# Two attention and expert layers on one core: other places for the first batches of the second attention, and the shared expert between the experts

## What is computed

```python
x = x + tanh(g_xattn[0]) * L0_xattn(layernorm(x), ctx)            # 16 heads of 8 rows, with projections
x = x + tanh(g_ffn[0])   * L0_ffn(layernorm(x))                   # 32 experts, 4 per token, 128 places each, and a shared one
x = x + tanh(g_xattn[1]) * L1_xattn(layernorm(x), ctx, ctx)       # 8 heads of 16 rows, no projections
x = x + tanh(g_ffn[1])   * L1_ffn(layernorm(x))                   # 8 experts, 2 per token, and a shared one
# L0_ffn: an expert takes at most 128 tokens
xe = zeros((E, CAP, D)).at[e_flat, pos].set(flat[tok], mode='drop')
h = relu2(einsum('ecd,ehd->ech', xe, up_w)); ye = einsum('ech,edh->ecd', h, down_w)
routed = (ye[e_flat, pos] * topk_w).reshape(T, K, D).sum(axis=1)
shared = relu2(hidden @ shared_up_w.T) @ shared_down_w.T
# L1_xattn
sm = softmax(einsum('bhdq,bhdl->bhql', qh, kh) * scale); ret = einsum('bhql,bhdl->bhdq', sm, vh)
```

## Time and profile before

| what | value |
|---|---|
| median of 3 runs | 784.0 us (779.7 to 788.89) |
| the profiled execution's own time | 784.32 us |
| its span in the trace | 782.5 us |
| TensorE busy, share of the span | 668.5 us, 85% |
| VectorE | 522.0 us, 67% |
| ScalarE | 378.4 us, 48% |
| GpSimd | 321.2 us, 41% |

### The profile page before, as it was taken

How to read it: one execution, slowest core, us unless ns; L and a number is a source line. 1 busy time by engine, 2 the same in 40 slices (tenths; PEclk the granted TensorE clock), 3 DMA queues, 4 the chain that set the end, 5 groups by cost and what they waited for, 6 DMA issues and landing times.

```text
span 782.5 us, 13620 instructions
## 1 busy us (share of the span) xinstructions
PE 668.5 (85%) x4737; PEld 349.8 (45%) x4738; DVE 522.0 (67%) x1252; ACT 378.4 (48%) x630; POOL 321.2 (41%) x337
## 2 busy tenths in 40 slices
PE   3899999999999899788646788799977999888896
PEld 1233333333333357567413344344423566666673
DVE  3889888888895798255267888796837733323236
ACT  2058878888776443243315566575502213333320
POOL 3534353534011101662578877621100057667430
PEclk9999999999999999799957999999999999999999
DMA  6834343544311700455346767786430022222127
GB/s 166 176 88 120 97 117 98 137 139 126 98 46 32 256 14 3 126 159 176 111 128 183 192 195 204 195 187 160 134 117 28 1 63 83 65 74 75 45 85 268
DMA packets 106362, 93.23 MB, mean 119 GB/s; under 512 B 25205, under 2 KB 92954, under 8 KB 106104
## 3 DMA queue, kind: packets, MB, share of 16 engines
q1 hardware_dynamic: 93600, 67.67, 31.6%
q0 software_dynamic: 8352, 18.74, 8.3%
q10 hardware_dynamic: 4344, 5.97, 2.8%
HBM read 50.63 MB, written 16.01 MB: 85 GB/s over the span
## 4 chain that ended last, share of the span: by engine, by line
PE 56%; DVE 14%; issue 11%; POOL 10%; DMA 4%; ACT 2%; SPq 2%; another core or an unknown queue 0%; ACTq 0%; POOLq 0%; DVEq 0%
PE O L443 9%; PE S L400 9%; POOL spare L266 6%; PE ST L1543 6%; DVE mx L562 4%; PE ST L939 2%; PE ST L1469 2%; PE M L1560 2%; PE S L1560 2%; PE ST L408 2%; PE M L492 2%; POOL QKc L276 1%; POOL QKs L285 1%; PE M L485 1%; PE M L468 1%
## 5 line engine op out<-in xcount | busy, mean ns | idle before, releaser
L562 DVE TENSOR_REDUCE mx<-S 128x2 f32<-128x512 f32 x384 | 249.8, 683 | 40.3 <-PE S L400 38.0
L314 ACT ACTIVATE PX<-ST 128x1024 f32<-128x1024 f32 x192 | 196.2, 1024 | 102.6 <-PE ST L408 92.0
L400 PE MATMUL S<-QS 62*128 62x256 bf16 (+1 forms) x768 | 152.0, 294 | 48.3 <-DVE mx L562 32.4
L408 PE MATMUL ST<-QS 64*128 64x256 bf16 (+1 forms) x768 | 141.6, 279 | 2.3 <-issue 1.2
L443 PE MATMUL O<-PX,VA 128*32 128x256 f32 x1536 | 123.6, 395 | 1.8 <-DMA VA<-in_val 1.7
L400 PEld LDWEIGHTS S<-QS 62*128 62x128 bf16 (+1 forms) x768 | 47.5, 97 | 169.1 <-DVE mx L562 105.7
L266 POOL DMA_INDIRECT spare<-ye,GI x64 | 67.2, 1050 | 32.2 <-DMA ye<-QKc 16.3
L1654 POOL DMA_INDIRECT PX<-xn,TI x39 | 39.8, 1020 | 59.1 <-DVE K1n L1843 39.7
L1543 PE MATMUL ST<-EGU,Cb 128*128 x156 | 55.6, 480 | 8.2 <-ACT Cb L1611 5.9
L408 PEld LDWEIGHTS ST<-QS 64*128 64x128 bf16 (+1 forms) x768 | 53.7, 97 | 17.9 <-issue 10.6
L782 POOL DMA_INDIRECT PX<-xn,TI x32 | 33.9, 1061 | 60.9 <-DVE spare L1179 44.1
(11 more groups left out here) (302 smaller groups left out, 1103.0 us busy)
## 6 DMA issues: line engine op xcount, KB each, us to landing
QS<-QKs SPq DMA_DIRECT2D x177, 128.0 KB
EGU<-in_ew SPq DMA_DIRECT2D x16, 256.0 KB, 2.8
xn<-spare SPq DMA_DIRECT2D x8, 512.0 KB, 5.5
ye<-QKc SPq DMA_DIRECT2D x32, 128.0 KB
VA<-in_val SPq DMA_DIRECT2D x16, 256.0 KB
spare<-yt SPq DMA_DIRECT2D x16, 256.0 KB, 6.4
Cb<-in_ctx SPq DMA_DIRECT2D x31, 128.0 KB
on<-OS SPq DMA_DIRECT2D x27, 128.0 KB
```

The source lines that it names most:

```text
L314: e.activation(M["PX"][pair % 4][:, :], M["ST"][pair % 2][:, :], ACT.Exp, scale=A.scale).then_inc(A.exp, 1)
L400: got = e.matmul(M["S"][n % 2][:, 256 * a:256 * a + 256], QS[:, 0, 128 * a:128 * a + 128], QS[:, 1, :], start=True, stop=True)
L408: got = e.matmul(M["ST"][(NP * t + k // 2) % 2][:, 512 * u + 256 * a:512 * u + 256 * a + 256], QS[:, 1, 128 * a:128 * a + 128], QS[:, 0, : ...
L562: e.tensor_reduce(M["mx"][b % 2][:, :, A.row_of_max(head)], M["S"][n % 2][:, :].rearrange("p (a s) -> p a s", a=2), AX.X, ALU.max, negate= ...
```

## The change

1. **Shared expert.** `down` takes single batches. Batches 8 to 11 leave the place ahead of the expert loop, chunks and batches 12 to 15 the place behind it; they stand in the loop now, by the tables `DOWN_AT` and `HIDDEN_AT` (step x of the loop: what follows the transposes of x). They use other accumulator banks. The copies, relus and squares on ACT, the sum of the last four batches on DVE (`shared_added(3)`, L1284, until now in step 1 of the second attention) and the constant rows that SP loads follow them. `keys_part` on ACT moves from x = 14 and 20 to 18 and 23.
2. **First batches of the second attention.** Places of sums, statistics and norms of batches 2 to 6 come from tables; batches 2 and 3 are split by DVE and ACT, not by GpSimd (`aided`); the number of gathers per step is another one.
3. **Every batch of it.** ACT's first and second part move one pair earlier (m = 1 and 2 instead of 2 and 3). GpSimd's second subtraction moves ahead of the last gather of its half. SP spreads all six transfers before the row of maxima (except in steps -1 to 1, where the row goes first), and the reciprocals move on DVE from k = 0 to k = 4 of their step, on SP behind the row.

```diff
-        return {-5: 8, -4: 10, -3: 14, -2: 18, -1: 24, 0: 30, 1: 36}.get(t, ...)
+        return {-5: 8, -4: 10, -3: 16, -2: 20, -1: 24, 0: 28, 1: 34}.get(t, ...)
+    SUM = {2: -12, 3: -4, 4: 4, 5: 9, 6: 13}
+    STATISTICS = {2: -11, 3: -1, 4: 7, 5: 12}
+    NORM = {2: -9, 3: 0, 4: 8, 5: 13}
+    PARTS = {0: (-29, -28), 1: (-21, -20), 2: (-7, -5), 3: (3, 5)}
+    FIRST_PART = {3: 1, 4: 4, 5: 7}
+    SECOND_PART = {3: 2, 4: 5, 5: 8}
+    def sums_at(self, b):
+        at = self.SUM.get(b, 8 * (b - 5) + 3)
+        return (at, at, at) if b == 2 else (at, at + 1, at + 2)
...
+        rows_first = not A.first and -1 <= t <= 1
+        if rows_first:
+            shift_rows()
         if within(b1):
...
             for k in range(3 if b1 == 0 else 6):
                 spread(e, A, M, b1, k)
-                if k == 2 and within(b5):
+                if k == 2 and within(b5) and A.first:
                     reciprocals()
-                if k == 2 and within(b2) and not A.first:
-                    shift_rows()
...
+        if not A.first:
+            if within(b2) and not rows_first:
+                shift_rows()
+            if within(b5) and A.late(b5):
                 reciprocals()
...
-        split = within(b0) and not b0 < A.helped
+        split = within(b0) and not b0 < A.aided
...
-        for n in gathers[half:]:
+        for n in gathers[half:half + 1]:
             gather(n)
         if split:
             ...
             e.tensor_tensor(part_of(S, 2), Q[:, :, :], part_of(S, 1), ALU.subtract).then_inc(A.res2, 1)
+        for n in gathers[half + 1:]:
+            gather(n)
...
-                if m == 2:
-                    if within(b0):
...
+                for b in range(NB):
+                    Q, S = M["QKc"][b % 2], M["QKs"][b % 2]
+                    if NP * t + m == A.FIRST_PART.get(b, NP * (b - 4) + 1):
...
+                    if NP * t + m == A.SECOND_PART.get(b, NP * (b - 4) + 2):
...
-                if k == 0 and within(b5):
+                if k == (4 if A.late(b5) else 0) and within(b5):
                     reciprocals(b5)
...
+SHARED_LATE = 8
+DOWN_AT = {1: 8, 3: 9, 5: 10, 7: 11, 20: 12, 22: 13, 24: 14, 26: 15}
+HIDDEN_AT = {9: 12, 11: 13, 13: 14, 15: 15}
+def hidden_bank(M, n):
+    return M["BK"][3 + n % 2] if n < 12 else M["BK"][2]
+def down_bank(M, n):
+    return M["BK"][5 + n % 2 if n < SHARED_LATE else 2 if n % 2 else 7]
...
-    w.wait_ge(G.er, E0)
-    hidden(e, w, G, M, 12, 13, 14, 15)
-    w.wait_ge(G.ey, E0)
-    down(e, w, G, M, 3)
-    w.wait_ge(G.xs, NB)
...
-    down(e, w, G, M, 2)
...
+        if x in DOWN_AT:
+            down(e, w, G, M, DOWN_AT[x])
+        if x in HIDDEN_AT:
+            hidden(e, w, G, M, HIDDEN_AT[x])
```

More of the change, by code:

```diff
@@ L105, in __init__ @@
         self.k0, self.sp0 = (0, 0) if self.first else (2, 96)
+        self.aided = 1 if self.first else 4
         self.s0 = 0 if self.first else 2
@@ L203, in attention_sp @@
                 spread(e, A, M, b1, k)
-                if k == 2 and within(b5):
+                if k == 2 and within(b5) and A.first:
                     reciprocals()
-                if k == 2 and within(b2) and not A.first:
-                    shift_rows()
             if b1 == 0 and behind_first:
                 behind_first()
-        else:
-            if within(b5):
+        elif within(b5) and not A.late(b5):
+            reciprocals()
+        if not A.first:
+            if within(b2) and not rows_first:
+                shift_rows()
+            if within(b5) and A.late(b5):
                 reciprocals()
-            if within(b2) and not A.first:
-                shift_rows()
         if within(b4):
@@ L578, in parts @@
     def parts(b, k):
-        n = 2 if A.first else 1
+        n = 1 if b < A.helped and not A.first else 2
         Q, S = M["QKc"][b % 2][:, 0:n, :], M["QKs"][b % 2][:, :, 0:n, :]
@@ L638, in attention_dve @@
             else:
-                if k == {-2: 5, -1: 1}.get(t, 0) and within(bn):
-                    statistics(bn)
-                if k == 0 and within(b5):
+                n = H * t + k
+                for b in range(NB):
+                    if n == A.STATISTICS.get(b, H * (b - 4)):
+                        statistics(b)
+                if k == (4 if A.late(b5) else 0) and within(b5):
                     reciprocals(b5)
@@ L742, in ffn0_sp @@
                 got.then_inc(G.late, 16)
+        if x in (18, 19):
+            w.wait_ge(G.up, 4 * NGRP)
+            for got in holes(e, M, d, x - 18, 1536, 2048):
+                got.then_inc(G.late, 16)
         if x >= PLACES - 4:
@@ L746, in ffn0_sp @@
         w.wait_ge(G.sty[k], 16 * E0 // 4)
-def ffn0_sp_later(e, w, G, M, d):
-    w.wait_ge(G.up, 4 * NGRP)
-    for n in range(2):
-        for got in holes(e, M, d, n, 1536, 2048):
-            got.then_inc(G.late, 16)
 def ffn0_pool_meanwhile(e, w, G, M):
@@ L859, in hidden, with down @@
         w.wait_ge(G.xt, 2 * g + 2)
-        w.wait_ge(G.relu, n - 1)
+        if n < 12:
+            w.wait_ge(G.relu, n - 1)
+        else:
+            w.wait_ge(G.relu, n)
+            w.wait_ge(G.xs, 12)
         for a in range(2):
-            got = e.matmul(M["BK"][3 + n % 2], M["SU"][:, a, 128 * c:128 * c + 128], M["XT0"][:, a, 512 * g:512 * g + 512],
+            got = e.matmul(hidden_bank(M, n), M["SU"][:, a, 128 * c:128 * c + 128], M["XT0"][:, a, 512 * g:512 * g + 512],
                            start=(a == 0), stop=(a == 1))
         got.then_inc(G.up, 1)
-def down(e, w, G, M, g):
-    w.wait_ge(G.sq, 4 * g + 4)
-    for b in range(GB):
-        n = GB * g + b
+def down(e, w, G, M, *batches):
+    for n in batches:
+        g, b = n // GB, n % GB
+        w.wait_ge(G.sq, 4 * g + 4)
         w.wait_ge(G.xs, n - 1)
+        if n >= SHARED_LATE:
+            w.wait_ge(G.sig, 2)
+            w.wait_ge(G.dve, G.at["TI"])
+        if n >= 12:
+            w.wait_ge(G.relu, 16)
         for c in range(4):
-            got = e.matmul(M["BK"][5 + n % 2][:, 0:256], M["RLs"][(4 * g + c) % 6][:, 128 * b:128 * b + 128], M["SD"][:, c, :],
+            got = e.matmul(down_bank(M, n)[:, 0:256], M["RLs"][(4 * g + c) % 6][:, 128 * b:128 * b + 128], M["SD"][:, c, :],
                            start=(c == 0), stop=(c == 3))
@@ L1284, in shared_added @@
     e.tensor_tensor(x, x, y, ALU.add).then_inc(G.xa, 1)
-def ffn0_dve_later(e, w, G, M):
-    def at(t, k):
-        if t == 1 and k == 6:
-            shared_added(e, w, G, M, 3)
-    return at
 def ffn0_dve(e, w, G, A, B, M, step):
@@ L1315, in ffn0_dve @@
             shared_added(e, w, G, M, 2)
+        if x == E0 - 3:
+            shared_added(e, w, G, M, 3)
         if x < E0:
```

101 lines of the change are left out of this document (49 added, 52 removed).

## The result

| | before | after |
|---|---|---|
| median of 4 runs each | 786.4 us (779.7 to 789.5) | 798.1 us (789.4 to 801.7) |
| profiled execution | 784.3 us | 800.1 us |
| ratio after / before, 95% interval | | 1.0141 [1.0081, 1.0202] |

The account below looks back on a forecast made before the run. No engine was taken to bound the kernel throughout; PE had 56% of the chain that ended last. 784.3 + 4 (shared expert) + 1 (attention until 505 us) - 3.5 (end) = 785.8, so 786 us; eight-in-ten range 771 to 797 us.

Parts of the forecast that it names:

- part 1: Shared expert's work moved into the expert loop: +4 us, bounds -1 to +21.
- The gathers ahead set the pace here, not PE; I take 0: Loop's first eight experts: 6.9 us of inserted PE work costs 0, bounds -3.8 to +4.9.
- first stretch: Expert loop's first eight experts, 314.01 to 331.48 us: four batches bring 6.9 us of PE work, taken as 0.
- gaps and slow clock: Loop's first eight experts: 8.7 of 17.5 us, which the new PE work was let use.
- My remark on the clock: Loop, 324 to 334 us: work in gaps may hold PE at 2.4 GHz; half of 7.66 us, 3.8.
- 2 us taken for the start: Ahead of the loop: it could start up to 6.9 us earlier but then waits for gathers; 2 us counted.
- second stretch: Expert loop, 19 experts from 331.48 to 363.40 us: 14.0 us of new work costs +3, bounds +3.0 to +14.0.
- DVE's sum and the end: DVE's sum of the last four batches, at x = 29 ahead of a square PE waits for: +1, 0 to 2.
- the gaps come back: Loop rival: PE does inserted work on top, +14 and 796 us; decides against the kernel from about +10; chance 0.18.
- Parts 2 and 3: Second attention's start and later steps, until 505 us: +1 us, bounds -10 to +7.5.
- parts 2 to 4: Second attention's start, later steps and end together: -2.5 us, own range -8 to +3.
- Part 4: End, after 505.8 us: DVE's waits for `dn`, 4.6 us, go away; -3.5 us, 0 to -6.

Follow-up runs that it names:

- groups 1 and 3: Follow-up runs on two chips, each timed beside the kernel before (785.1 and 783.7 us); they include the shared-expert change alone and the whole change.
- e14_waits_again: Kernel before plus the shared-expert change alone and 96 already raised waits near the start of ACT's program, run again on another chip: 794.7 us, one run.
- e13_reload_later: Kernel before with its five reloads of expert weights issued 14 experts later: 782.7 us, ratio 1.0044.
- e18_no_reload: Kernel before without its five reloads of expert weights: 781.1 us, one run.
- e1_shared: Kernel before plus the shared-expert change alone: 792.5 us beside 785.1, ratio 1.0131.
- the doubled matmuls: Shared-expert change alone, plus matmuls of batches 8 to 11 repeated ahead of the loop, result unread: ratio 1.0166 to kernel before; again 774.6 us, one run.
- groups 1, 3 and 4: Three groups of follow-up runs, each on its own chip, with the kernel before timed beside them at 785.1, 783.7 and 780.7 us.
- groups 2 and 5: Two groups of follow-up runs, each on its own chip, with the kernel before timed beside them at 754.7 and 756.8 us.
- b0_before: Kernel before, unchanged, traced on the same chip as the changed kernel: 783.7 us.
- experiment 4: Shared-expert change alone in three variants (nothing inserted before expert 9, matmuls doubled, 96 waits on ACT) against the kernel before: ratios 1.0226, 1.0166, 1.0216.
- e7_late_from_6: Kernel before with only the second attention's late changes, from step 2 on (ACT's parts from batch 6): 748.5 us beside 754.7, ratio 0.9914.
- e12_waits: Kernel before plus the shared-expert change alone and 96 already raised waits near the start of ACT's program: ratio 1.0216.

## Why the prediction was wrong

**The step that failed** is in part 1: "The gathers ahead set the pace here, not PE; I take 0", with bounds of -3.8 to +4.9. Measured: **+6.0** in the first stretch, above the upper bound; +5.4 and +4.2 in the pairs of groups 1 and 3, near it; +6.7 on the chip without stops. So 4.2 to 6.7 of the 6.9 us put in came back. (In e14_waits_again, one run, it was only 1.3 to 2.0 more than in e13_reload_later and e18_no_reload beside it.) Three things were wrong in the step.
- I divided 17.5 us into work and 8.7 us of "gaps and slow clock" that inserted work could use. On chips of this kind most of it comes with the stops, for the same instructions take 10.3 us on the chip without them: ACT is late with its input ready, and then PE waits in the down product (L947 before, 4.3 + 3.2 us of its waits in the whole loop). The inserted batches stand between transposes and up product. In the profile of e1_shared PE is held for 3.54 us at a down product and does its batch 1.4 us behind that wait, not in it. That the order decides this I infer; a batch ahead of the down product wasn't tried.
- I costed a batch at 1.73 us. Taking the work away from ahead of the loop left PE waiting for gathers, and the first batch behind took 3.4. My remark on the clock had the sign wrong: I let work in the gaps hold the clock, but the same edit opened a gap ahead of it. On the chip without stops the doubled matmuls, which held the clock, gave back 2.3 us of 6.7; with stops this wasn't measured.
- "2 us taken for the start": the first transposes do stand 2.8 us nearer to the first gather (2.5 us after it, 5.3 before), and give it all back in the next wait.

**The rest of part 1.** The second stretch was too low as well: +4.4 for +3 in this pair (9.6 of the 14.0 us of new work were covered), +6.1 and +6.6 in the pairs of groups 1 and 3, where the loop of before is shorter there. DVE's sum and the end were +1.0 for +1 (0.3 and 0.9). Loop +11.3 for +4; the rival "the gaps come back" had +14 and 796 us, and its threshold of +10 is borne out. That 14.0 us of work left the place behind the loop was worth nothing, as said: the first scores stand 17.4 us after the first gather of `ye`, 17.9 before.

**Parts 2 and 3** were read rightly up to batch 4 and the steps behind it: GpSimd's two idle times, batch 4 2.6 us later for 2, GpSimd up to 8.7 us behind for 7.5, steps of 8.4 us as given, back to the end. The pairs of profiles give -1.4 and -3.0 us at the last row (I had +1 and -3.5 for the end). That agreement is partly luck: over the seven profiles of this kind of chip with the attention of before, the last row stands at 175.1 to 180.4 us, and the three with the new one have 176.5 to 177.1, so single profiles show no gain. In time parts 2 to 4 measured +0.4% [0.05, 0.81], 3 us slower, where I had -2.5; which term is off by that much stays open. The up to 3.2 us that gathers might lose beside DVE's new subtractions didn't come: the three gathers beside batch 2's took 1.00 to 1.19 us, and batch 3's fell into GpSimd's idle time.
**Part 4**: the waits for `dn` are gone.
**The bound** of 771 to 797 us missed by 1 us; with +6 in the first stretch the sum is 791.8. The rest, to the 800.1 of the profiled execution, is the late stage's clock (4.1 us, it differs from run to run), 1.4 ahead of the first gather, 1.4 in the second stretch and 1.1 at the last row. A second measurement of the pair had +1.0% [0.55, 1.48], inside the range as a ratio. The chance of 0.27 for slower by over 1% was too small for a loop whose waits I couldn't name.

## What to carry to other kernels

A gap can take new work only if it opens where that work stands in the engine's order; before filling one, name what the engine waits for on each side of it, and on which instruction. Work that is moved away also moves its cover: here it had kept TensorE's clock up ahead of the loop, and moving it won 2.8 us for the first transposes and nearly nothing for expert 8. And where two edits each shorten a stage, look for the place where one is queued behind the other: late steps of 8.4 us instead of 9.3 were worth nothing until the transfers of batches 3 and 4 no longer stood behind a row on SP, or batch 4's part behind an exponential; then 0.9 and 0.7%.

## What the runs showed of the hardware

The kernel before took 781 to 785 us beside groups 1, 3 and 4, and 755 to 757 beside groups 2 and 5. Each group had its own chip and no chip came twice, so the difference may lie in the chip or in the time of measuring; I call it the chip's. In the profiles the difference is in two stages: the first expert loop (64 to 67 us against 54 to 55) and what follows the second attention (224 to 233 against 212 to 215). In the loop it shows as several stops between 319 and 332 us in which ACT starts 1 to 2 us after its input is ready (some 4 in the changed kernel), with TensorE at 0.50 to 0.60 of its clock from 324 to 334 us instead of 1.00. The stops came whether or not weights were reloaded there, and with 96 waits ahead of them in ACT's program the first one stayed where it was. This is the loop of before on a chip with stops (b0_before), from 324 to 334 us; the same stretch without stops is the second row of the windows in experiment 4 above (e7_late_from_6), 9.04 us of PE work at clock 1.00:

```profile
324.00:334.00 10.00, 6.75 (x27) 5.24 (x27) 3.00 (x8) 2.56 (x9) 5.90 (x6) 0.56 0.45 135
```

So a gap read in one profile can be the chip's, and an edit that fills it costs more where it isn't there: part 1 made the loop 11 to 12 us longer with stops (8 in the run with 96 waits) and 16.0 without. In time that is 1.3% (e1_shared) against 2.2% (e12_waits), with intervals that still overlap.
